# Transformer layer on one core: value projections ahead of the attention, first scores in slot 0, and LoRA folds on host-turned weights that pass through three engines

## The reference

```python
xn = _layernorm(x, axis=-1)
q = jnp.dot(xn, Wq) ; kv = jnp.dot(xn, Wkv)
scores = jnp.einsum('bhqd,bhkd->bhqk', q, k)
scores = jnp.where(causal[None, None], -jnp.inf, scores)
weights = jax.nn.softmax(scores * (1.0 / HD ** 0.5), axis=-1)
s = jnp.dot(ctx, Wo) + bo
gate = _matmul_lora(xn, gate_w, gate_a, gate_b)
up = _matmul_lora(xn, up_w, up_a, up_b)
g = _silu(_matmul_lora(jax.nn.silu(gate) * up, down_w, down_a, down_b))
x = x + s * g
```

## Time and profile before

| | us |
|---|---|
| median of 3 runs | 984.64 (982.81 to 989.12) |
| the profiled execution, its own time | 989.02 |
| span of its trace | 987.3 |
| PE busy | 927.0 (94%) |
| PE weight loads busy | 598.5 (61%) |
| DVE busy | 576.7 (58%) |
| ACT busy | 487.5 (49%) |
| POOL busy | 318.1 (32%) |
| mean granted TensorE clock | 0.977 |

### The profile page before, as it was taken

One profiled execution on the slowest core, in us unless ns is written; L12 is line 12 of the kernel. 1 busy time (PEld: TensorE's weight loads), 2 busy tenths in 40 slices (PEclk: granted clock), 3 DMA queues, 4 the chain that ended last, 5 costly groups with the idle time before them and its releaser, 6 DMA issues.

```text
span 987.3 us, 18068 instructions
## 1 busy us (share of the span) xinstructions
PE 927.0 (94%) x6599; PEld 598.5 (61%) x6599; DVE 576.7 (58%) x1659; ACT 487.5 (49%) x978; POOL 318.1 (32%) x320
## 2 busy tenths in 40 slices
PE   2797999999999999999999999999999999999986
PEld 2665667676766676767676766554555555555764
DVE  6755666666666666666666666676566656530025
ACT  2432556565656565656565656555444434435211
POOL 4022234343535352525252525330213122120126
PEclk9899999999999999999999999989999999999998
DMA  9456242424242424242424243367565454534454
GB/s 293 132 186 206 64 136 80 133 83 134 82 134 83 133 83 125 86 124 88 119 89 124 93 127 101 101 186 195 166 169 146 124 158 122 139 105 135 144 150 150
DMA packets 142934, 129.02 MB, mean 131 GB/s; under 512 B 36176, under 2 KB 104368, under 8 KB 142624
## 3 DMA queue, kind: packets, MB, share of 16 engines
q1 hardware_dynamic: 142848, 127.87, 43.6%
HBM read 74.07 MB, written 53.22 MB: 129 GB/s over the span
## 4 chain that ended last, share of the span: by engine, by line
PE 84%; DVE 8%; ACT 3%; DMA 2%; issue 2%; POOL 0%; SPq 0%; POOLq 0%; DVEq 0%; ACTq 0%
PE bank L934 24%; PE o L1071 12%; PE bank L246 9%; PE s L1035 9%; PE st L1054 9%; PE bank L247 7%; PE bank L248 7%; DVE junk L1516 2%; PE bank L896 2%; DVE neg_pad L1532 1%; PE bank L909 1%; PE bank L913 1%; DVE hid L1406 1%; DMA inv_sums<-scratch_r 1%; ACT gate L1168 1%
## 5 line engine op out<-in xcount | busy, mean ns | idle before, releaser
L1297 ACT ACTIVATE prob<-st 128x512 f32<-128x512 f32 (+1 forms) x640 | 324.3, 554 | 287.7 <-PE st L1054 287.1
L1516 DVE CUSTOM_DVE_ANT_0 junk<-s,mask 128x128 bf16<-128x128 f32 (+3 forms) x512 | 229.3, 487 | 116.3 <-PE s L1035 115.5
L1519 DVE TENSOR_REDUCE part_max<-s 128x1 f32<-128x512 f32 x256 | 163.8, 681 | 103.9 <-PE s L1035 103.7
L503 POOL TENSOR_SCALAR_AFFINE_SELECT prob<-prob 128x512 f32<-128x512 f32 x128 | 82.3, 655 | 262.1 <-ACT prob L1297 261.6
L1035 PE MATMUL s<-k,q 64*128 64x512 f32 (+3 forms) x768 | 150.0, 379 | 10.5 <-DVE part_max L1516 8.5
L934 PE MATMUL bank<-x_hi,w_hi 64*128 64x512 f32 (+1 forms) x704 | 150.9, 415 | 2.4 <-DVE hid L1406 1.1
L1071 PE MATMUL o<-prob,v 128*32 128x512 f32 (+3 forms) x1536 | 145.3, 497 | 0.0
L934 PE MATMUL bank<-x_lo,w_hi 64*128 64x512 f32 (+1 forms) x704 | 142.9, 391 | 0.0
L934 PE MATMUL bank<-x_hi,w_lo 64*128 64x512 f32 (+1 forms) x704 | 142.2, 389 | 0.0
L1054 PE MATMUL st<-q,k 64*128 64x512 f32 (+3 forms) x768 | 137.2, 375 | 3.9 <-ACT prob L1297 3.8
L512 POOL TENSOR_TENSOR tanh<-tanh,hid 128x512 f32<-128x512 f32 (+1 forms) x44 | 56.5, 1285 | 166.4 <-DVE hid L1406 166.4
(11 more groups left out here) (121 smaller groups left out, 1014.6 us busy)
## 6 DMA issues: line engine op xcount, KB each, us to landing
hid_in<-scratch_hid SPq DMA_DIRECT2D x16, 1408.0 KB, 7.4
q<-scratch_q SPq DMA_DIRECT2D x60, 200.0 KB
scratch_hid<-tanh_hid_hi SPq DMA_DIRECT2D x40, 256.0 KB, 2.1
scratch_hid<-hid_lo SPq DMA_DIRECT2D x40, 256.0 KB, 2.4
scratch_o<-o_sb SPq DMA_DIRECT2D x32, 256.0 KB
scratch_q<-proj_hi SPq DMA_DIRECT2D x30, 256.0 KB
k<-scratch_k SPq DMA_DIRECT2D x30, 192.0 KB
ctx<-scratch_o SPq DMA_DIRECT2D x16, 256.0 KB, 3.9
```

The costliest lines, as they stand in the source:

```text
L503: ins = pool.affine_select(out=blk, in_=blk, compare_op=ALU.is_ge, fill=0.0, base=0, pattern=[[0, REP], [1, P]], channel_multiplier=-1)
L1297: nc.scalar.activation(prob[:, job % 3, h, 0:JOB_COLS[j]], st[at % ST_BANKS][:, 0:JOB_COLS[j]], ACT.Exp, scale=float(HD) ** -0.5).then_inc ...
L1516: ins = dve.tensor_tensor_reduce(junk[:, n % S_BANKS, 0:wd], bank_[:, 0:wd], mask[:, C - wd:C], 1.0, LOWEST, ALU.add, ALU.max, part[:, h, ...
L1519: ins = dve.tensor_reduce(part[:, h, qt, dst:dst + 1], bank_[:, 0:wd], AX.X, ALU.max)
```

## The change

1. **Order of the background.** `value(c)` stands before the projections for c=2 and 3, and `value` of c=0, 1 belongs to `LEAD`, so it is through before slot 0. The two folds of h=0 stand before the `AFTER` projection. The sum of `LEAD` and `EARLY` is the same.
2. **First scores.** Group 0 spreads its maxima from slot 0 over 45 slots.
3. **ACT and DVE in the head.** ACT does the splits of all `LEADING` projections first, then the four `xT` copies of c=1, `root(3)` and `split_low_b`. DVE does `layernorm(3)` behind all `LEADING` low projections. `split_low_a` waits for the x_lo of c=3 and no longer for the value stores; the first `split_weight` now has that wait.
4. **Weights turned by the host**, before launch. `fold` is 4 matmuls of the LoRA part over two steps, `fold_down` one matmul. The 88 transposes of L909 and the 44 of L948 are gone.
5. **The fold over three engines.** DVE adds bank and raw tile in place in the ring (`add_weight`, `add_down`), which frees the bank; ACT rounds from the ring; POOL subtracts (`low_weight`, `low_down`, 22 and 11 new instructions), each some steps later. DVE's own `low_weight` and `low_down` are gone. A ring slot is now free at `w_lo` or `d_lo`; SP's loads of the raw tiles stand later accordingly. `down(0)` waits for `d_lo` tile by tile.

The core of the diff (`...` marks what is left out):

```diff
+FIRST_OF_ALL, FIRST_SLOTS = 0, 45
...
             yield "turn", c, k
+        yield "value", c, 0
         yield ("proj", *BESIDE[c])
         yield "proj", c, KEYS_BLOCK
-        yield "value", c, 0
+    for i in range(2):
+        yield "fold", 0, i
     for c, blk in AFTER[:SOON]:
         yield "proj", c, blk
-    for i in range(2):
-        yield "fold", 0, i
...
-LEAD = sum(STEPS[kind] for (kind, *_), u in NUMBER.items() if u <= NUMBER["proj", 1, 0])
-EARLY = NUMBER_STEPS["fold", 0, 1] - FIRST_HIDDEN - LEAD
+LEAD = sum(STEPS[kind] for (kind, *_), u in NUMBER.items() if u <= NUMBER["value", 1, 0])
+EARLY = NUMBER_STEPS[("proj", *AFTER[SOON - 1])] - FIRST_HIDDEN - LEAD
...
+            def low_weight(h, i):
+                n = 2 * h + i
+                pool.wait_ge(w_hi, n + 1)
+                pool.tensor_tensor(wl[:, h % 2, i, :, 0:rows[h]], raw_tile(n), wh[:, h % 2, i, :, 0:rows[h]],
+                                   ALU.subtract).then_inc(w_lo, 1)
+
+            def low_down(h):
+                hp = rows[h]
+                pool.wait_ge(d_hi, h + 1)
...
+                        if c == 1 and h + 1 < NH:
+                            yield 3 * STEPS["fold"]
+                            low_weight(h + 1, 0)
+                            yield STEPS["proj"] - STEPS["fold"]
+                            low_weight(h + 1, 1)
...
             def fold(h, i):
-                pe.wait_ge(raw_landed[n % 8], DMA * (n // 8 + 1))
                 pe.wait_ge(low_lo, 2)
                 out_ = take_bank(("fold", h, i))
                 for kt in range(KT):
-                    pe.matmul(out_[:, kt * P:kt * P + hp], ring[0:hp, n % 8, kt * P:(kt + 1) * P], ident[0:hp, 0:hp],
-                              is_transpose=True, start=kt == 0, stop=False, skip_group_check=True)
-                yield 1
-                for kt in range(KT):
                     mm = pe.matmul(out_[:, kt * P:kt * P + hp], a_gu[:, i, kt * P:(kt + 1) * P],
-                                   bT[:, i, h * P:h * P + hp], start=False, stop=kt == KT - 1, skip_group_check=True)
-                mm.then_inc(filled, 1)
-                yield 1
+                                   bT[:, i, h * P:h * P + hp], start=True, stop=True)
+                    if kt == KT - 1:
+                        mm.then_inc(filled, 1)
+                    if kt % 2:
+                        yield 1
...
             def down(t):
-                pe.wait_ge(d_lo, NH)
...
                 for h in range(NH):
                     hp = rows[h]
+                    if t == 0:
+                        pe.wait_ge(d_lo, h + 1)
...
             def split_low_a():
-                for i in range(2):
-                    act.wait_ge(v_stored[i], DMA * NCH // 2)
-                act.wait_ge(xn_ready, NCH)
+                act.wait_ge(xT_lo_late, 2 * KT)
...
             def split_weight(h, i):
+                if n == 0:
+                    for odd in range(2):
+                        act.wait_ge(v_stored[odd], DMA * NCH // 2)
+                act.wait_ge(w_sum, n + 1)
+                nc.scalar.activation(wh[:, h % 2, i, :, 0:rows[h]], raw_tile(n), ACT.Copy).then_inc(w_hi, 1)
...
-                    if c == 1 and blk == KEYS_BLOCK:
-                        root(3)
-                        split_low_b()
-                        for kt in range(KT):
-                            copy_x(1, kt)
                     yield STEPS["proj"]
                     split_projection(c, blk)
+                for kt in range(KT):
+                    copy_x(1, kt)
+                root(3)
+                split_low_b()
...
-            def low_weight(h, i):
...
+            def add_weight(h, i):
+                key, n = ("fold", h, i), 2 * h + i
+                dve.wait_ge(raw_landed[n % 8], DMA * (n // 8 + 1))
+                wait_filled(dve, key)
+                dve.tensor_tensor(raw_tile(n), folded(key), raw_tile(n), ALU.add).then_inc(w_sum, 1)
...
                     low_projection(c, blk)
-                    if (c, blk) == (0, 0):
-                        layernorm(3)
+                layernorm(3)
```

More of the change, by code:

```diff
@@ L228, in stream_slots @@
             g, w = divmod(n, NU)
-            even = SLOTS * g + FIRST_UNIT + UNIT_SLOTS * sum(weight[:w]) // sum(weight)
+            first, width = (FIRST_UNIT, UNIT_SLOTS) if g else (FIRST_OF_ALL, FIRST_SLOTS)
+            even = SLOTS * g + first + width * sum(weight[:w]) // sum(weight)
             even -= even % 2
@@ L442, in wait_filled, with raw_tile, folded @@
             engine.wait_ge(filled, NUMBER[key] + 1)
+        def raw_tile(n):
+            return ring[:, n % 8].rearrange("p (k h) -> p k h", k=KT)[:, :, 0:rows[n // 2]]
+        def folded(key):
+            return bank_of(key)[:, :].rearrange("p (k h) -> p k h", k=KT)[:, :, 0:rows[key[1]]]
         def projection(c, blk):
@@ L550, in background @@
                 low_query_weights(3)
+                yield NUMBER_STEPS["fold", 0, 1] - done
+                done = NUMBER_STEPS["fold", 0, 1]
+                for i in range(2):
+                    low_weight(0, i)
                 for h in range(NH):
@@ L635, in load_raw @@
                 elif before >= 0:
-                    wait_filled(sp, ("fold", *divmod(before, 2)))
+                    sp.wait_ge(w_lo, before + 1)
                 if n < RAW_LOW:
                     h, i = divmod(n, 2)
-                    dst, src = ring[0:rows[h], n % 8], raw_weights[i][h * P:h * P + rows[h]]
+                    dst, src = raw_tile(n), raw_weights[i][h, :, :, 0:rows[h]]
                 elif n < RAW_DOWN:
@@ L990, in background @@
                         yield from turn_x(c, kt)
+                    yield from value(c)
                     yield from project(*BESIDE[c])
                     yield from project(c, KEYS_BLOCK)
-                    yield from value(c)
+                for i in range(2):
+                    yield from fold(0, i)
                 for c, blk in AFTER[:SOON]:
                     yield from project(c, blk)
-                for i in range(2):
-                    yield from fold(0, i)
                 for h in range(NH):
@@ L1173, in split_down @@
             def split_down(h):
-                key = ("down_fold", h, 0)
-                wait_filled(act, key)
-                nc.scalar.activation(dh[0:rows[h], h], bank_of(key)[0:rows[h], :], ACT.Copy).then_inc(d_hi, 1)
+                hp = rows[h]
+                act.wait_ge(d_sum, h + 1)
+                nc.scalar.activation(dh[0:hp, h], ring[0:hp, (RAW_DOWN + h) % 8], ACT.Copy).then_inc(d_hi, 1)
             def split_wo(kb):
@@ L1236, in background @@
                     split_projection(c, KEYS_BLOCK)
-                    yield STEPS["value"]
-                    copy_value(c)
                 split_low_a()
+                for i in range(2):
+                    yield STEPS["fold"]
+                    split_weight(0, i)
                 for c, blk in AFTER[:SOON]:
@@ L1242, in background @@
                     split_projection(c, blk)
-                for i in range(2):
-                    yield STEPS["fold"]
-                    split_weight(0, i)
                 for h in range(NH):
@@ L1461, in background @@
                     low_projection(c, KEYS_BLOCK)
-                    yield STEPS["value"]
                 low_of_low(1, a_gu, a_raw, slice(BESIDE_ROWS, 2 * BESIDE_ROWS))
+                for i in range(2):
+                    yield STEPS["fold"]
+                    add_weight(0, i)
                 for c, blk in AFTER[:SOON]:
@@ L1466, in background @@
                     low_projection(c, blk)
-                for i in range(2):
-                    yield STEPS["fold"]
-                    low_weight(0, i)
                 for h in range(NH):
```

102 lines of the change are left out of this document (49 added, 53 removed).

## The result

The changed kernel is slower: 1006.07 us as the median of 6 runs, where the kernel before had 986.64 on the same chip; ratio 1.0193, 95% interval 1.0167 to 1.0219. The forecast was 971.2 us, faster. The profiled execution has 1006.25 us and a span of 1004.4, 17.1 more than before. Of the runs further down, one of the four timed executions of `relay_only` took 4452.07 us, unlike any other on record, and is left out of its ratio.

The account below looks back on a forecast made before the run. PE was taken to bound the hidden stage, partly the down folds, with waits counting at 90 to 105 us. Gains of 1.7 + 8.2 + 3.5 = 13.4 us took 984.64 to 971.2 us, range 963 to 979.

Parts of the forecast that it names:

- Hidden stage: 105 to 600 us: fewer PE matmuls at the folds gain 0.82 us per period, 8.2 us over 10 periods.
- The price of a matmul: Hidden stage folds: one transpose or LoRA matmul costs 0.10 us on PE from start to start.
- Down folds: 650 to 680 us: 44 transposes go, worth 6.8 us; half taken as gain, 3.5 us.
- the gaps on PE that the prediction names: Down folds: every second gap on PE belongs to ACT or DVE, so only part of 6.8 us comes through.
- rival A: Only the hidden stage pays; layernorm(3), bT and exps behind down_hi replace the other gains; 976.4 us, chance 0.24.
- The tail: After the down folds: down(0) waits tile by tile, the last relay behind 10 others; no cost.
- Head: Up to the hidden stage: 3.5 - 1.4 - 0.7 + 0.3 = 1.7 us gain, from -1 to 4.5.
- the wait before the first fold: Stall at 90 us: folds need low_a on DVE, so PE idles 2.8 us.
- the exp wait: Head: a wait of about 3 us on PE before the second pair of st.
- 0.5 us for the rest: Stall at 90 us: one long gap becomes two shorter and some transposes go, given +0.5 us.
- Rival B: Clock also returns in the down folds, 2.6 us more, and the head gives 4.5; 965.8 us, chance 0.20.
- Rival C: POOL's new subtracts stretch DVE's neg_pad twice a period, 19.6 us slower; 990.8 us, chance 0.05.

Follow-up runs that it names:

- relay_only: Host-turned weights and the fold over three engines alone, on the kernel before, with its old head; ratio 1.0180 to the kernel before.
- filler run: Changed kernel with four unused identity transposes put back on PE in each fold and each down fold; ratio 1.0121 to the kernel before.
- down_even: Changed kernel with ACT's rounding of the down folds, and POOL's subtract with it, one step later; ratio 1.0148 to the kernel before.
- The filler on top of it: down_even plus four unused identity transposes in each fold and down fold; down folds 27.4 us, ratio 1.0021 to the kernel before.
- head_only: Kernel before with the new head alone, weights still turned on PE and folds as before; ratio 1.0036 to the kernel before.
- low_a alone: Kernel before with only ACT's split of low_a no longer waiting for the value stores; ratio 0.9954 to the kernel before.
- values ahead alone: Kernel before with the earlier low_a split, new ACT and DVE lead order, and values of c=2 and 3 ahead of their projections; ratio 1.0081.
- head_slot6: New head on the old folds, with the first scores from slot 6 over 39 slots as before; ratio 1.0051 to the kernel before.
- after: The changed kernel itself, all five parts, against the kernel before; median 1006.07 us, ratio 1.0193.

## Why the prediction was wrong, point by point

- **Hidden stage, 8.2 us.** The price of a matmul, 0.10 us, was right: the LoRA matmuls cost from start to start what was worked out (0.36 to 0.37 for two; four took 0.73 with a gap, not 0.60). The step that failed is the sentence that the gain is PE's "as long as no other engine becomes late", which was then tested with DVE's 63% and ACT's 58% over the whole stage. In the four slots of the folds DVE has three pairs of maxima and two adds, with no pause behind the first, and PE was already in step with it. The gain there is 0.25 us a period instead of 0.82, and the clock, for which the sum had no term in this stage, takes 1.5 back in six of ten. The filler run shows that work on PE at this place keeps the clock at 2.4 GHz: it puts some back, and all ten periods are at 1.00.
- **Down folds, 3.5 us.** They lost 5.3. The earlier trace rows do not show the gaps on PE that the prediction names; PE's waits there came to 3.3 us, all on ACT or DVE. Half of the transposes' price was taken as gain, because DVE has 22.00 us of work. The list of costs counted the relay's durations and not its place: the sentence of rival A, that exps stand behind `down_hi`, was the mechanism, but with a price of nothing gained instead of a loss. down_even measured 4.4 us for one step. The filler on top of it brings the clock to 1.00 and the stretch from 33.1 to 27.4 us (from 31.4 in the two other executions of that stage). The tail was put at nothing, since `down(0)` waits tile by tile; it costs 1.3 us in the changed kernel.
- **Head, 1.7 us.** It lost 5.1. Values from 38.97 and the second pair of scores at 51.24 came as forecast (39.1 and 51.1), the wait before the first fold was 2.88 (2.8), the exp wait 2.07 (3). Wrong was their worth: the early start ran into waits for q (2.73), for maxima (2.7 and 1.2) and for x copies (1.8 and 0.5), and two stretches at half clock, 49 to 61 and 96 to 108 us. By the sum of waits over 0.2 us PE stood 13.9 us from 38 to 112 where it stood 11.8. The step that failed is the pricing: the term counts the waits that go and come, and 0.5 us for the rest. The same head, with the same waits, ended at 106.6 us in down_even: 4.5 of the 5.1 us lie within what the length of the slow stretches does from one execution to the next. That the new head loses at all is shown by the timed runs of head_only, about 3.5 us. low_a alone is a gain (4.3 us in the head). The values ahead alone are a loss by the loads; with values in the lead and the first folds ahead of AFTER as well (head_slot6) the head came to 108.5 and not to 114.5. Slot 0 and the place of the first folds were each undone, and neither gave the loss back by the timed runs. Values in the lead were not varied alone. How the 3.5 us are made up stays open.
- **Rival B** had the clock's sign wrong. It took the half clock in the down folds for something that goes away when the four transposes of a fold do; they went, and the clock of that stretch fell from 0.83 to 0.66. **Rival C**, the slower one, had 0.05, and its condition did not come about: `neg_pad` is as before (176 ns at the median of all 32, 1164 at worst), because none of the 33 new subtracts runs beside one. The traces do show the hold that it was read from. In both kernels 12 of the 32 `neg_pad` take 1.12 to 1.16 us, each starts while POOL's add of `hid` (L514 before, L526 after) runs and ends 0.03 us behind it, and the 20 that take 0.17 to 0.18 us run beside nothing on POOL. Eleven of PE's 12 waits behind `neg_pad` follow a stretched one, 0.32 to 0.61 us each, so a stretch of 0.98 costs PE about a third of that, where C's price took all of it; the twelfth, 2.0 us, follows a short one. No run moved that add. The Trainium skill's rule ("SBUF — State Buffer", Who interferes with whom), that VectorE and GpSimd shut each other out at their shared port, agrees with these 12 and cost nothing new here; `add_weight`, with one input in PSUM, took 0.68 us, as said. The rival that was missing is the one that held in the hidden stage: less work for PE, so a slower PE.

## What to carry to other kernels

Before work is taken from the busiest engine, read the slots it is taken from, not the stage's averages: if another engine has no pause in those very slots, the gain is idle time, and on TensorE it can be followed by a slower clock, as in six of ten periods here. In a relay, in which engines hand a tile on and each works its stream in order, the place can count more than the duration; a step that lands between two instructions whose pair is waited for is paid by the waiter. A change of several parts should be timed part by part: here one of them, a wait less, was worth 0.46% and was buried under the others. And a stretch of a few us at half clock that comes and goes between executions of the same instructions should be looked for before a difference of a few us is given a cause.

## What was not expected of the hardware

Delays of about 0.2 us each between matmuls, in four consecutive slots, were followed by some 3 us at the 1.2 GHz level in 6 of 10 periods of the same instructions, and in the other four by none; two unused transposes a fold kept it at 2.4 GHz in ten of ten, and so did putting a projection between the two folds. The same instructions of the head ended at 106.6 us in one execution (down_even) and at 111.1 in another (after). The Trainium skill ("TensorE: Matmul & The Clock Gate", A second HAM failure mode: psum-queue depth-cycling) tells of a kernel in which small idle pieces between groups of matmuls let the clock go to and fro. The runs here agree: 0.98 in the hidden stage of the kernel after, with delays of 0.2 us at the folds, and 1.00 with the filler. The forecast did not weigh it.
